# Softmax denominators from sums over four key tiles instead of two, and the copies and scalings moved around them

## What is computed

```python
g = (t @ gw.T + gb)[:, None, :];  b = (t @ bw.T + bb)[:, None, :]
h = g * x * rsqrt(mean(x * x, -1) + EPS) + b
q, k, v = (h @ W.T).reshape(B, 1024, 16, 32)        # for Wq, Wk, Wv
attn = einsum('blhd,bmhd->bhlm', q, k) / sqrt(32)
p = softmax(attn, axis=-1)
o = einsum('bhlm,bmhd->blhd', p, v).reshape(B, 1024, 512)
x = x + o @ Wo.T
x = x + (silu(h2 @ gate_w.T) * (h2 @ hid_w.T)) @ out_w.T    # h2: the same norm of the new x
```

## Time and profile before

| | |
|---|---|
| median of 3 runs | 2507.95 us (2507.72 to 2508.66) |
| profiled execution, its own time | 2508.16 us |
| its span in the profile | 2506.1 us |
| mean granted clock of TensorE | 0.983 |
| busy PE / DVE / ACT / POOL | 2375.7 / 1661.6 / 1308.1 / 1145.1 us |
| attention, first to last instruction | 0 to about 1485 us |

### The profile page before, as it was taken

How to read it: one execution, slowest core, us unless ns; L and a number is a source line. 1 busy time by engine, 2 the same in 40 slices (tenths; PEclk the granted TensorE clock), 3 DMA queues, 4 the chain that set the end, 5 groups by cost and what they waited for, 6 DMA issues and landing times. The chain is left out here.

```text
span 2506.1 us, 39896 instructions
## 1 busy us (share of the span) xinstructions
PE 2375.7 (95%) x11396; PEld 1578.2 (63%) x11396; DVE 1661.6 (66%) x2732; ACT 1308.1 (52%) x2287; POOL 1145.1 (46%) x1095
## 2 busy tenths in 40 slices
PE   5999999999999999999999957999999999999999
PEld 4655436554447554456544436888888888888887
DVE  4766735666725666527667436887688778877877
ACT  3366762566762556743667724446344544454454
POOL 0265661456650565532556634641473157216711
PEclk8999999999999999999999978999999999999999
DMA  5212203212122122132122053115411541254125
GB/s 191 66 40 61 58 22 107 50 40 68 47 71 66 35 68 50 48 94 51 39 55 57 30 168 126 60 55 168 166 55 60 180 151 52 68 169 152 51 77 175
DMA packets 92670, 209.75 MB, mean 84 GB/s; under 512 B 15632, under 2 KB 15632, under 8 KB 90640
## 3 DMA queue, kind: packets, MB, share of 16 engines
q1 hardware_dynamic: 91344, 202.71, 27.1%
q0 software_dynamic: 1088, 4.19, 0.5%
HBM read 134.23 MB, written 19.92 MB: 62 GB/s over the span
## 5 line engine op out<-in xcount | busy, mean ns | idle before, releaser
L418 POOL TENSOR_TENSOR sums<-probs 128x512 f32<-128x512 f32 x512 | 648.4, 1292 | 708.2 <-ACT probs L567 706.7
L641 DVE TENSOR_REDUCE pmax<-bank 128x1 f32<-128x512 f32 x1024 | 654.2, 684 | 280.6 <-PE bank L854 272.5
L567 ACT ACTIVATE probs<-bank 128x512 f32<-128x512 f32 x1024 | 584.7, 597 | 371.6 <-PE bank L938 338.6
L938 PE MATMUL bank<-qs,ks 128*128 128x512 f32 x1024 | 458.6, 452 | 28.5 <-ACT probs L567 27.8
L938 PEld LDWEIGHTS bank<-qs,ks 128*128 128x128 f32 x1024 | 190.9, 187 | 372.0 <-ACT probs L567 226.6
L854 PE MATMUL bank<-ks,qs 96*128 96x512 f32 x1024 | 398.1, 401 | 4.0 <-DVE pmax L641 3.6
L1501 PE MATMUL bank<-H_hi,wt_hi 128*128 128x512 f32 x896 | 349.9, 390 | 14.6 <-DVE H_lo L1356 14.6
L1515 PE MATMUL bank<-ow,aw 128*128 128x512 f32 x1536 | 358.7, 392 | 0.0
L1501 PE MATMUL bank<-H_lo,wt_hi 128*128 128x512 f32 x896 | 349.5, 390 | 0.0
L1501 PE MATMUL bank<-H_hi,wt_lo 128*128 128x512 f32 x896 | 349.5, 390 | 0.0
L1515 PEld LDWEIGHTS bank<-ow,aw 128*128 128x128 f32 x1536 | 285.6, 188 | 59.9 <-issue 1.2
(11 more groups left out here) (136 smaller groups left out, 3139.1 us busy)
## 6 DMA issues: line engine op xcount, KB each, us to landing
raw<-in_gu_w SPq DMA_DIRECT2D x66, 512.0 KB, 3.6
wo_raw<-in_out_w SPq DMA_DIRECT2D x128, 256.0 KB, 2.6
ks<-qk_hi SPq DMA_DIRECT2D x136, 128.0 KB, 2.4
qs<-qk_hi SPq DMA_DIRECT2D x264, 64.0 KB, 2.0
x<-in_x SPq DMA_DIRECT2D x10, 1024.0 KB, 5.1
ks<-qk_lo SPq DMA_DIRECT2D x68, 128.0 KB, 2.4
qs<-qk_lo SPq DMA_DIRECT2D x132, 64.0 KB, 2.0
wv<-wv_parts SPq DMA_DIRECT2D x4, 2048.0 KB, 9.1
```

What stands on the lines that cost most here:

```text
L418: nc.gpsimd.tensor_tensor(sums[:, h, :], probs[:, 0, h, :], probs[:, 1, h, :], ALU.add) \
L567: nc.scalar.activation(probs[:, s % 2, h, :], sbank[i % SB][:], ACT.Exp, scale=SCALE).then_inc(st_done, 1)
L641: nc.vector.reduce_max(pmax[:, t, h, hf:hf + 1], mbank[n % MB][:], AX_X).then_inc(sq_done, 1)
L938: nc.tensor.matmul(sbank[i % SB][:], ks[:, g % 2, h, s * P:(s + 1) * P], qs[:, u % 3, h, :], start=True, stop=True).then_inc(st_ready, 1)
```

## The change

- A quad of four key tiles is added up instead of a pair: at s % 4 = 1 POOL adds the two tiles in `probs`, at 2 and 3 it adds the new tile to `sums` in place. So POOL makes 24 adds a unit instead of 16, and PE two denominator groups instead of four. They stand at (5,1) of the unit and (1,1) of the next.
- ACT's exponentials wait for the adds of two tiles before (except at s % 4 = 3, where the wait is already implied).
- `values` moves to h = 3, 1, 3, 2 for s % 4 = 0, 1, 2, 3.
- The copy of the unit's output on ACT moves from (1,0) to (0,3).
- The scaling of the next batch's x at (4,6) and (6,7) moves from DVE to ACT.
- At the batch's end the last denominator group follows the second output product instead of the first, and DVE copies the first product out before it splits operands 2 and 3 and inverts the denominators.

```diff
-PAIRS = 4
+QUADS = 2
+QT = 4
+VALUES_AT = (3, 1, 3, 2)
+SUMS_AT = {(5, 1): (0, 0), (1, 1): (1, 1)}
-SUMS = PAIRS * GH
+SUMS = QUADS * (QT - 1) * GH
...
+def sums_done(b, u, s, h):
+    return b * (NU * SUMS) + (SUMS * (u + 1) + GH * (s // QT * (QT - 1) + max(s % QT, 1) - 1) + h + 1)
+def products_done(b, u, quad):
+    return b * (NU * QUADS) + (QUADS * u + quad + 1)
+def sums_at(u, s, h):
+    back, quad = SUMS_AT.get((s, h), (NU, 0))
+    return (u - back, quad) if u >= back else None
...
-                        for h in range(GH if s % 2 else 0):
+                        for h in range(GH if s % QT else 0):
                             pool.wait_ge(st_done, SCORES_T(b, NT + n * GH + h + 1) + SB)
-                            if h == 0:
-                                pool.wait_ge(d_ready, products_done(b, u, s // 2))
-                            nc.gpsimd.tensor_tensor(sums[:, h, :], probs[:, 0, h, :], probs[:, 1, h, :], ALU.add) \
+                            if s % QT == 1 and h == 0:
+                                pool.wait_ge(d_ready, products_done(b, u, s // QT))
+                            if s % QT > 1:
+                                pool.wait_ge(sum_done, sums_done(b, u, s - 1, h))
+                            first = probs[:, 0, h, :] if s % QT == 1 else sums[:, h, :]
+                            nc.gpsimd.tensor_tensor(sums[:, h, :], first, probs[:, s % 2, h, :], ALU.add) \
                                 .then_inc(sum_done, 1)
...
+            def scale_x(b, hf, t):
+                act.wait_ge(inv_ready, b * 2 + 3 + hf)
+                nc.scalar.activation(x4[:, t, :], x4[:, t, :], ACT.Copy, scale=inv[:, t:t + 1]).then_inc(x_scaled, 1)
...
-                            if s % 2 == 0:
-                                act.wait_ge(sum_done, sums_done(b, u, s // 2 - 1, h) if s
-                                            else sums_done(b, u - 1, PAIRS - 1, h))
+                            if s % QT != QT - 1:
+                                act.wait_ge(sum_done, sums_done(b, u, s - 2, h) if s >= 2
+                                            else sums_done(b, u - 1, NS + s - 2, h))
                             nc.scalar.activation(probs[:, s % 2, h, :], sbank[i % SB][:], ACT.Exp,
                                                  scale=SCALE).then_inc(st_done, 1)
+                            if (u, s) == (4, 6):
+                                scale_x(b, 0, h)
+                            if (u, s) == (6, 7):
+                                scale_x(b, 1, h)
...
-                            if (s, h) == (1, 0) and u:
+                            if (s, h) == (0, GH - 1) and u:
                                 output(b, u - 1)
                             if (s, h) == (1, 2) and u:
                                 denominators(b, u - 1)
...
-                            if (u, s) == (4, 6):
-                                scale_x(b, 0, h)
-                            if (u, s) == (6, 7):
-                                scale_x(b, 1, h)
...
-                for t in range(3):
+                for t in range(2):
+                    lo_part(t)
+                out_tile(0)
+                for t in range(2, 4):
                     lo_part(t)
                 for part in range(3):
                     normalise(b, NU - 1, part)
-                for t in range(NT):
+                for t in range(1, NT):
                     out_tile(t)
...
-                            if h == 2 + (s + 1) % 2 and (u or s):
+                            if h == VALUES_AT[s % QT] and (u or s):
                                 values(b, u if s else u - 1, (s - 1) % NS)
-                                if s % 2 == 0:
-                                    denominators(b, u if s else u - 1, (s // 2 - 1) % PAIRS)
+                            if sums_at(u, s, h):
+                                denominators(b, *sums_at(u, s, h))
...
-                    if t == 0:
-                        denominators(b, NU - 1, PAIRS - 1)
+                    if t == 1:
+                        denominators(b, NU - 1, QUADS - 1)
```

More of the change, by code:

```diff
@@ L130 @@
 SCORES_Q = Counter(0, NU * NMAX + NT)
-SUMS = PAIRS * GH
-assert 2 * PAIRS == NS
+SUMS = QUADS * (QT - 1) * GH
+assert QT * QUADS == NS
 LINKS_PER_BATCH = NU * (2 + 2)
@@ L365, in _ @@
                 hold(sp, held, pv_done, b * (NU * NS) + NU * NS + 2)
-                hold(sp, held, sum_done, sums_done(b, NU - 1, PAIRS - 1, GH - 1))
+                hold(sp, held, sum_done, sums_done(b, NU - 1, NS - 1, GH - 1))
                 load_wv()
@@ L505, in denominators @@
             def denominators(b, u):
-                act.wait_ge(d_ready, products_done(b, u, PAIRS))
+                act.wait_ge(d_ready, products_done(b, u, QUADS))
                 act.wait_ge(on_done, b * NU + (u + 1))
@@ L615, in scale_x @@
             def scale_x(b, hf, t):
-                n = hf if b is None else b * 2 + 2 + hf
+                n = hf
                 dve.wait_ge(inv_ready, n + 1)
@@ L856, in max_tile, with denominators @@
                                  start=True, stop=True).then_inc(sq_ready, 1)
-            def denominators(b, u, pair):
-                pe.wait_ge(sum_done, sums_done(b, u, pair, GH - 1))
-                if pair == 0:
+            def denominators(b, u, quad):
+                pe.wait_ge(sum_done, sums_done(b, u, QT * quad + QT - 1, GH - 1))
+                if quad == 0:
                     pe.wait_ge(od_act, b * (2 * NU) + (2 * u + 2))
                 for h in range(GH):
-                    last = nc.tensor.matmul(dbank[DH * h:DH * h + DH, :], ones[:], sums[:, h, :], start=(pair == 0),
-                                            stop=(pair == PAIRS - 1))
+                    last = nc.tensor.matmul(dbank[DH * h:DH * h + DH, :], ones[:], sums[:, h, :], start=(quad == 0),
+                                            stop=(quad == QUADS - 1))
                 last.then_inc(d_ready, 1)
```

## The result

The changed kernel takes **2519.2 us** (median of 6, 2516.4 to 2522.2) against 2507.8 (6 runs, 2506.0 to 2509.0): ratio **1.0045, 95% interval 1.0033 to 1.0058**, 11 us slower. The forecast was 2489.5 with a range of 2460 to 2512: the time moved the other way and lies above the range. The profiled execution of the changed kernel was its slowest, 2522.2.

What follows compares the result with a forecast made beforehand. It took PE to bound attention, 95% busy, with slots without projection paced by the round trip through ACT's exponentials. Terms summed to -4.6 us a batch, -18.4 in all, taking 2507.95 to 2489.5, range 2460 to 2512.

Steps and rivals of the forecast that it cites:

- D group: Denominator products on PE, 0.86 us each; four a unit become two, 64 groups fewer: minus 13.8 us a batch.
- scaling on ACT: Scaling the next x on ACT at (4,6) and (6,7): plus 3.0 us a batch, bounds 0.6 and 4.8.
- POOL's chain: POOL's adds, wait for the product and hand-over take 16.3 us per quad, so POOL should not set the pace.
- Rival (c): POOL sets the pace: products at (1,1) and (5,1) wait for its last add; 2571 us at 1.5 an add; chance 0.06.
- Wait 2: ACT's copies at (1,2) lose the value group's cover, 0.9 or 0.5 us a unit: 5.1 a batch, bounds 0 and 8.5.
- value copies: At (0,3) the output's copy is done before the value products at (1,1); PE's wait mostly goes: minus 1.2 a batch.
- Wait 1: Exponentials wait for POOL's first adds, 0.5 us in second quads of units 0, 2, 4, 6: 2.0 a batch.
- Batch end: A new wait of some 2 us before product 2 replaces one before product 5: plus 0.3, bounds 0 and 2.2.
- Rival (b): The waits take all the gain: half as dear again gives 2510 us; one more clock fall a batch adds 6; chance 0.18.

Runs made afterwards that it cites:

- the short first pass: The changed kernel with the first pass of adds of each quad over 64 of the 512 columns: 2505.4 us, ratio 1.0001.
- the run with D one slot earlier: The changed kernel with value groups of odd tiles back at h = 2 and denominator groups at (1,0) and (5,0): 2491.5 us, ratio 0.9935.

## Why the prediction was wrong

The mechanism was right in the main: the groups pay, POOL has the time, and nearly every wait that I named is there. What failed is the size of four terms, all in one direction: the price of a D group, the wait for ACT's copies, the wait for POOL's first pass and the scaling on ACT. By the steps of the prediction:

- **Minus 13.8 a batch for the D groups**: 11.7 measured (46.6 of 55.0), 0.73 a group instead of 0.86. I read the price in unit 1, where it holds, and used it in all units; in 4 and 5 two groups give 0.9 and 1.2 and not 1.7.
- **POOL's chain**: right. 1.28 an add in place too, PE never waited for it, POOL idled 165 us waiting for D. Rival (c) did not happen.
- **Wait 2 and the value copies**: I had 5.1 - 1.2 = 3.9 a batch; the move measured alone costs **5.9**. The copies at (1,2) came to less than forecast: 0.94 in units 1, 3, 5 and 6 as I had it, but 0.24 in units 2 and 4 and nothing in unit 7. The wait for the value copies went away, and unit 7's first quad got 0.7 shorter for it. What I had left out is the work behind (5,2): I did not go through it, and there PE stands 1.0 us before S(6,1) in unit 5 and 1.2 at (6,0) in unit 7.
- **Wait 1**: in the units that I named, except unit 4; 2.0 a batch forecast, 2.8 measured by the short first pass. I priced PE's wait for the exponentials and left out the maxima rows queued behind them on ACT.
- **Scaling on ACT**: 3.0 forecast, **4.6** measured alone, with the fall of the clock in it. I took DVE as a place where it "held up nobody much" and never asked what DVE's scaling would meet under the new stream of adds.
- **Batch end**: +0.3. A gap of 2.05 us before product 2 in place of one of 1.9 to 2.9 before product 5, as forecast; the run with the old order shows no difference clear of the noise.

| us in all four batches | forecast | measured |
|---|---|---|
| D groups | -55.2 | -46.6 |
| wait 2 and value copies | +15.6 | +23.6 |
| wait 1 | +8.0 | +11.0 |
| scaling on ACT | +12.0 | +18.3 |
| batch end | +1.2 | in the noise |
| sum | -18.4 | +6.3 |

The changed kernel itself is at +11.3. Wait 1 was measured in the changed kernel and the others in the kernel before, each with an interval of 3 to 4 us to either side, so their sum is uncertain by some 7 (estimate), and the 5 us that are left are not shown to be anything. The sum is 25 us above the forecast's; no term makes the difference alone. The D groups gave 9 less than forecast, the values cost 8 more, the scaling 6 more and wait 1 3 more; the forecast had left only 18 of gain. Rival (b) had this case, waits "half as dear again", at 2510, with a second fall of the clock as 6 more: 2516. I gave it 0.18 and ended the range at 2512.

The clock is in these terms and not beside them. The waits at the border cost more than their own length: the granted clock over the 23 us around it was 0.73 to 0.79 instead of 0.93. What that is worth can be bounded: over unit 7 of the third batch the clock took 0.16 of 38.4 us instead of 0.05 of 36.2, so at most 4.3 us a batch (estimate), less what PE spent waiting in that time. The clock is not the whole loss: the run with D one slot earlier still has 0.86 to 0.91 over unit 7 and is 16 us faster than the kernel before.

## What to carry to other kernels

A group of PE work that "only costs time" may be the cover under which another engine does its copies; before removing or moving it, list everything the other engines do in the slots behind it, also in the units that differ from the one read. When one engine is made busy without pauses, look for work of other engines that lived in its pauses: here an inverse root and four scalings, which a tile earlier no longer held up PE. And when several waits are estimated in a schedule with no slack, they can err together: here wait 1, the scaling and the moved values came out 1.4 to 1.5 times as dear, and the gain 0.85 times as large, so the range should reach that far.

## What the runs showed that I had not expected

- Four DVE scalings of 128x512 took 1.67 us with POOL idle, 5.73 beside POOL's back-to-back adds; POOL's adds stretched far less (eight in 10.59 us against 9.97, the median of eight unbroken ones in the changed kernel).
- The position of two of the eight value groups of a unit, each moved by one slot, is worth 24 us in either kernel.
- Behind PE waits of 0.3 to 1.2 us in close succession the granted clock at the unit border was 0.73 to 0.79 over 23 us, where it had been 0.93; with the late scaling gone it was 0.93 to 1.00 again (0.85 once).
- The same unit of the kernel before takes 36.2 us at a granted clock of 0.95 and 34.5 us at 1.00.
